# Half of two small tile loads moved from SyncE's queue to ScalarE's queue, in the column stage of a two-layer graph kernel

## What is computed

```python
# x is (5120, 64), adj is (5120, 5120), all float32
u = par_u[0] * par_u[1] * (diag_u[:, None] * x[:2048] @ W_u) + x[:2048]
i = par_i[0] * par_i[1] * (diag_i[:, None] * x[2048:] @ W_i) + x[2048:]
e = concatenate([u, i])
h = adj @ (adj.T @ e)
x = layernorm(x + layernorm(h) * gamma + beta + x)
T1 = adj @ x;  T2 = 2 * adj @ T1 - x;  T3 = 2 * adj @ T2 - T1
x = layernorm(x + x @ w[0] + T1 @ w[1] + T2 @ w[2] + T3 @ w[3] + bias)
```

## Time and profile before

| | before |
| --- | --- |
| median of 3 runs | 1223.32 us (1223.15 to 1223.8) |
| the profiled execution, its own time | 1222.88 us |
| its span, first to last instruction | 1221.1 us |
| PE busy | 1109.2 us (91%) |
| DVE busy | 928.5 us (76%) |
| ACT busy | 332.0 us (27%) |
| POOL busy | 257.0 us (21%) |
| HBM read | 348.97 MB, 287 GB/s over the span |

### The profile page before, as it was taken

The page is one execution under the profiler, slowest core; times in us unless marked ns, Lnnn a source line. Parts: engine busy times, 40 slices in busy tenths (PEclk is TensorE's granted clock), DMA queues, the critical chain, the costliest instruction groups (busy, mean ns, idle before and its releaser), DMA issues.

```text
span 1221.1 us, 13860 instructions
## 1 busy us (share of the span) xinstructions
PE 1109.2 (91%) x4995; PEld 480.7 (39%) x5004; DVE 928.5 (76%) x960; ACT 332.0 (27%) x594; POOL 257.0 (21%) x420
## 2 busy tenths in 40 slices
PE   4999999999999996899889999999899999598794
PEld 3444454444454442444333333444344443122221
DVE  2698798999998998698777766665666667588784
ACT  1456456466465562400100000000100000011010
POOL 0476555463453543100000000000000000011111
PEclk9999999999999998899999999999999999799898
DMA  7999999999999975899999999999999999999991
GB/s 225 301 291 299 278 299 305 297 295 282 300 274 288 282 206 121 181 291 309 238 347 347 337 313 308 306 293 255 262 331 333 325 305 328 348 311 342 352 353 33
DMA packets 372731, 350.82 MB, mean 287 GB/s; under 512 B 11613, under 2 KB 371333, under 8 KB 372693
## 3 DMA queue, kind: packets, MB, share of 16 engines
q1 hardware_dynamic: 259092, 237.35, 69.6%
q10 hardware_dynamic: 110880, 110.11, 31.6%
q0 software_dynamic: 2720, 2.86, 1.0%
HBM read 348.97 MB, written 1.31 MB: 287 GB/s over the span
## 4 chain that ended last, share of the span: by engine, by line
PE 54%; DVE 13%; SPq 12%; ACT 10%; ACTq 5%; issue 4%; DMA 1%; POOL 0%; DVEq 0%
PE bank L1176 30%; ACT terms L775 9%; SPq L337 7%; ACTq L279 5%; SPq L326 4%; DVE turned L496 4%; PE bank L1227 4%; PE bank L1189 3%; PE bank L1006 2%; PE bank L1046 2%; PE bank L1034 2%; PE bank L1018 2%; PE bank L1058 2%; DVE shared L516 2%; DVE xq L496 1%
## 5 line engine op out<-in xcount | busy, mean ns | idle before, releaser
L1176 PE MATMUL bank<-turned,terms 128*128 128x512 f32 x680 | 301.6, 596 | 4.8 <-DVE turned L496 3.3
L386 POOL COPY raw<-raw 32x512 f32<-32x512 f32 x320 | 194.2, 607 | 239.6 <-DVE raw L533 190.2
L516 DVE STREAM_TRANSPOSE shared<-shared 32x512 f32<-32x512 f32 x320 | 224.0, 700 | 4.1
L1006 PE MATMUL bank<-shared 128*64 128x256 f32 x1600 | 206.4, 385 | 6.9 <-DMA shared<-in_adj 6.9
L496 DVE STREAM_TRANSPOSE turned<-raw 128x2048 f32<-128x2048 f32 x72 | 165.1, 2301 | 58.3 <-PE bank L1176 49.5
L496 DVE STREAM_TRANSPOSE turned<-shared 128x2048 f32<-128x2048 f32 x68 | 156.1, 2303 | 60.6 <-PE bank L1176 46.4
L775 ACT COPY terms<-terms 32x512 f32<-32x512 f32 x320 | 197.0, 616 | 8.3 <-issue 3.2
L1176 PEld LDWEIGHTS bank<-turned,terms 128*128 128x128 f32 x680 | 126.6, 190 | 170.9 <-issue 163.3
L431 POOL DMA_DIRECT2D out<-scratch x40 | 21.7, 549 | 681.3 <-DVE scratch L725 681.2
L1006 PEld LDWEIGHTS bank<-shared 128*64 128x64 f32 x1600 | 112.0, 136 | 88.2 <-issue 32.6
L1069 PE MATMUL bank<-turned,t_quart 128*64 128x512 f32 x160 | 82.7, 603 | 8.5 <-DVE t_quart L540 8.5
(11 more groups left out here) (143 smaller groups left out, 1060.2 us busy)
## 6 DMA issues: line engine op xcount, KB each, us to landing
shared<-in_adj SPq DMA_DIRECT2D x100, 1024.0 KB, 10.8
raw<-in_adj SPq DMA_DIRECT2D x106, 512.0 KB, 10.6
raw<-in_adj ACTq DMA_DIRECT2D x106, 512.0 KB, 12.4
shared<-in_adj SPq DMA_DIRECT2D x104, 512.0 KB, 10.6
shared<-in_adj ACTq DMA_DIRECT2D x104, 512.0 KB, 12.6
raw<-in_adj SPq DMA_DIRECT2D x80, 256.0 KB, 7.6
xq<-in_x POOLq DMA_DIRECT2D x40, 32.0 KB, 6.2
out<-scratch POOLq DMA_DIRECT2D x40, 32.0 KB, 5.2
```

The source lines that it names most:

```text
L386: last = nc.gpsimd.tensor_copy(moved[Q32 * c:Q32 * (c + 1), :, :, Q32 * q:Q32 * (q + 1)], beside[Q32 * q:Q32 * (q + 1), :, c, :, :])
L516: last = nc.vector.transpose(low_turned[Q32 * c:Q32 * (c + 1), :, :, Q32 * q:Q32 * (q + 1)], low[Q32 * q:Q32 * (q + 1), :, :, Q32 * c:Q32 ...
L1006: last = nc.tensor.matmul(t_bank[H * odd:H * (odd + 1), 0:PW], e[:, s * SB + b, :], panels[slot][:, s * SB + b, :], start=(k == 0 and b < ...
L1176: last = nc.tensor.matmul(sum_bank[parity][:, :], terms[:, c * GB + i, columns], turned[place][:, i * BANK:(i + 1) * BANK], start=(first a ...
```

## The change

SP loads only the pieces q = 0 and 1 of each tile (partitions 0 to 63). The pieces 3 and 2 are issued by ScalarE's queue, in a new function `load_upper`. Before the loop ScalarE issues them for both tiles of the first pair, between the table load and panel 1. In the loop it issues them for both tiles of the next pair, behind the t copy of the even panel, after a wait on `tile_turned` for the tiles of the pair that is being used up. The counts that VectorE waits for are the same. `tile_rows` is moved up, so that both queues' code sees it.

```diff
--- before.py
+++ after.py
@@ -279,6 +279,8 @@
             queue.dma_start(pairs[u % SLOTS][Q32 * q:Q32 * (q + 1), :].rearrange("p (b n) -> p b n", b=GB * NQ),
                             rows_of[:, :, at_column:at_column + SPAN * P]).then_inc(pair_loaded[u % SLOTS], DMA)
 
+        tile_rows = adj.rearrange("(g b i) c -> g i b c", b=BANK // Q32, i=Q32)
+
         def by_chunk(a, width):
             return a.rearrange("p (k f) -> p k f", f=width)
 
@@ -316,13 +318,11 @@
 
             seg_rows = adj.rearrange("(s b p) c -> s p b c", p=P, b=SB)
 
-            tile_rows = adj.rearrange("(g b i) c -> g i b c", b=BANK // Q32, i=Q32)
-
             def load_layer0_tile(k, last, column):
 
                 if last is not None:
                     sp.wait_ge(tile_turned, last + 1 + RAW)
-                for q in (0, 2, 1, 3):
+                for q in (0, 1):
                     sp.dma_start(raw[k][Q32 * q:Q32 * (q + 1), :].rearrange("p (b c) -> p b c", c=P),
                                  tile_rows[2 * SEGS[k] + 1][:, :, bass.ds(column + P * q, P)])\
                         .then_inc(raw_loaded[k], DMA)
@@ -796,9 +796,22 @@
 
             act.wait_ge(ident_made, 2)
             nc.scalar.activation(stats[:, 1, 0:1], ident[:, 0:1], ACT.Sqrt)
+            def load_upper(k, last, column):
+
+                if last is not None:
+                    act.wait_ge(tile_turned, last + 1 + RAW)
+                for q in (3, 2):
+                    act.dma_start(raw[k][Q32 * q:Q32 * (q + 1), :].rearrange("p (b c) -> p b c", c=P),
+                                  tile_rows[2 * SEGS[k] + 1][:, :, bass.ds(column + P * q, P)])\
+                        .then_inc(raw_loaded[k], DMA)
+
+            for k in range(TILED):
+                load_upper(k, None, 0)
             layer0_panel(1, 1)
             with act.Fori(1, NJ // 2) as two:
                 layer0_panel(0, two * 2)
+                for k in range(TILED):
+                    load_upper(k, (two - 1) * TILED + k, two * BANK)
                 layer0_panel(1, two * 2 + 1)
 
             def take_h(n, s):
```

## The result

The change makes the kernel **slower**: 1237.72 us (median of 13 runs, 1228.07 to 1245.48) against 1224.22 us (13 runs, 1222.56 to 1226.54), a ratio of 1.0106 with a 95% interval of 1.0081 to 1.0131. The prediction was 1221.2 us with a range to 1226.2; the result lies outside it, on the other side.

A forecast was written before the change was run, and what follows sets the result against it. It took the column stage's early panels to be bound by DMA engines running behind, later ones by TensorE and ScalarE in turn. Settled lateness falling from 38.54 to 36.4 us took 2.1 off 1223.32: 1221.2 us, range 1220.2 to 1226.2.

The forecast's parts named there:

- A few us at most: Column stage: the change can only win back early transfer waits, 6.6 us in panels 1 to 6.
- the longest hold: Start of ScalarE's queue: bound with the longest issue, 5.2 us, giving panel 1 a lateness of 38.7, in all 1223.3 us.
- rival C: In the loop, ScalarE's issues hold it past the slack in every pair: 8 us slower, 1229.5 us; chance 0.15.
- the term for half a tile beside segments, 1.51 us: Early panels: two pieces, 524 KB, move beside SP's segments at 349 GB/s together, 0.88 us less than alone.
- rival B: Early panels: no overlap, panel 5 gets a half more ahead, 1225.3 to 1225.7 us; sign: panels 3, 5 later; chance 0.20.
- the prediction's terms for panels 1, 3 and 5: Lateness, t copy time minus 22.09 us per panel, from bytes ahead: 35.70, 35.32 and 35.27 us.
- ScalarE's hold at the start: Before the loop, four issues end at 41.96, so the first L766 copies and TensorE run 2.9 us late.
- the forecast's 36.4 for panel 1: Panel 1's lateness with the start's hold, 33.5 + 2.9; the largest term, so it sets the settled lateness, 38.54 before.
- the slack of 5.9: In the loop, the queue may hold ScalarE for 5.9 us after an even panel's t copy at no cost.
- A sign of being wrong in the reasons: Column stage: panel 1's copy isn't the one held back, or L1006 still waits for transfers in panels 5 and 6.
- should read near 349: Early stage: windows in which tile pieces run were to read near 349 GB/s and not 193.
- A: Column stage: the forecast as summed, with overlap, 2.1 us less, 1221.2 us (1220.4 to 1223.3 by hold); chance 0.50.

The follow-up runs named there:

- late: Tile 1's half issued behind the odd panel's t copy, against the change: 1253.92 us; the same with alternating pieces: 1229.66 us.
- amid the copies: Tile 1's half issued amid the odd panel's spread copies, against the change: 1232.44 us with alternating pieces, 1235.51 us with 0, 1 and 3, 2.
- one queue: SP issues all pieces in about the change's order, against the kernel before: 1244.58 us with 0, 1 and 3, 2; 1236.12 us alternating.
- the two named above: SP-only runs against the kernel before: pairs 0, 2 and 1, 3 one segment apart, 1233.87 us; 0, 1 and 3, 2 in the change's order, 1244.58 us.

## Why the prediction was wrong

**Right: the bound and the ceiling.** "A few us at most" holds (4.1 us with the tiles nearly gone), the settled pace didn't move, and what hurts in the change hurts in the first panels. Some bounds of the rivals are off by 0.1 to 0.2 us (38.54 - 35.70 off 1223.32 is 1220.5, the longest hold gives 1223.5, rival C 1229.3); none of them changes the forecast.

**Wrong: the term for half a tile beside segments, 1.51 us.** It measured 2.87 in the change (2.39 was its price alone). The 347 GB/s of the earlier trace rows were two queues with 1 KB packets, each into another group of 32 partitions. Here 512 B packets ran beside 1 KB packets, and the packet counts say what that gives: 3438 packets in 10 us of segments (row below), 344 per us, and 2814/8 = 352 per us with both queues. That is one large packet every 2.91 ns; of small ones alone one comes every 1/443 us = 2.26 ns (last section). Beside large ones a small one took 2.87/1043 us = 2.75 ns: none of its time was hidden behind the other queue's.

```profile
DMA packets 3438, 3.49 MB, mean 349 GB/s; under 512 B 60, under 2 KB 3435, under 8 KB 3435
```

The Trainium skill ("DMA: Bandwidth & Descriptors", Queues, rings and completion order) says that each DMA engine takes turns between the queues it has work for at packet granularity. The trace agrees that both queues move at once between 92 and 100 us. It doesn't show turns of one packet each (1770 and 1043), and at 484 to 489 us the second queue moved nothing. The same page's rule that spreading over queues gains no bandwidth (Rules for kernel authors), which I had set aside on the earlier trace rows, held here.

In the run with alternating halves the queues between 90 and 98 us read

```profile
q1 hardware_dynamic: 1791, 1.81, 81.6%
q10 hardware_dynamic: 1166, 0.58, 29.8%
```

or 8.0 - 1.81/0.349 = 2.81 us for 0.58 MB, 2.5 for a half (2.4 ns per packet). That is about the 2.39 of a half alone: rival B had the price, no overlap, nearly right. With 2.5 in place of 1.51 the prediction's terms for panels 1, 3 and 5 become 35.07 - 2.39 + 2 x 2.5 = 37.7, 36.45 - 3 x 2.39 + 4 x 2.5 = 39.3 and 38.16 - 5 x 2.39 + 6 x 2.5 = 41.2. That run has 37.50, 39.86 and 44.14: the one size put right gives panels 1 and 3 and leaves 2.9 us of panel 5, of which 1.7 are the low clock (below). In the change, with its 2.87, they become 38.4, 40.8 and 43.4 against 37.96, 43.66 and 51.24. Most of the growing rest is the next point.

**Wrong: a part of the change that no term covered.** The sum took the two pieces as two pieces, whichever. Going from 0, 2 and 1, 3 to 0, 1 and 3, 2 is 8.5 of the 13.5 us. Four pairs of runs that differ in nothing else show it beyond their intervals: 1237.7 and 1229.2 (both halves), 1227.7 and 1224.3 (tile 0), 1234.8 and 1227.0 (tile 1), 1253.9 and 1229.7 (late). Two more point the same way with intervals that overlap: 1235.5 and 1232.4 (amid the copies), 1244.6 and 1236.1 (one queue). The order alone, in the kernel before, costs 2.2 us. So *that* the order of pieces costs is shown; *why* is argued. That the partition halves 0 to 63 and 64 to 127 matter rests on rows of one stretch, 134 to 169 GB/s against over 182, and the alternating run on one queue has a low of 139. An open rival is what the pieces read: 0 and 1, and 3 and 2, are also neighbouring columns of the same rows of adj, and no run here changes which columns go to which partitions. For the partition halves the Trainium skill has a reason ("SBUF — State Buffer", Door 1: The DMA port swizzle): partitions 32 apart share a port and partitions 64 apart don't, so a transfer to 64 neighbouring partitions reaches no more ports than one to 32. By it pieces 0 and 1 queue at the same eight ports. The rates of that stretch fit, but no run here shows a port.

**Wrong: the price of an order.** The sum and rival B counted the bytes ahead of a segment. ScalarE's pieces overtake part of SP's backlog, so their place by issue says little (early 1229.2, late 1228.9). Pieces right behind a segment seem to delay it too (55.02 for 52.87, in one comparison), and on one queue pieces between segments cost 9 us that no count of bytes gives.

**Missed: what a long wait costs behind it.** Behind TensorE's longer waits the granted clock often read 0.50 for some 3 us: in the change at 43 to 46 us behind the wait of 2.20, at 101 to 104 behind 2.63, and at 153 to 158 with waits of 2.64 and 2.50; in its alternating version at 149 to 152 behind 2.17. Not always: behind that version's wait of 2.30, at 101.83, it stayed at 1.00. It costs only where no later wait takes it up, on the last segment of a panel: 1.5 us in the change and 1.7 in its alternating version (148.61 to 154.59, 5.98 for 4.29), both in panel 5. The kernel before has no such stretch between 57 and 170 us. In the one-queue run, behind a wait of 4.14 us, it is the lower level too:

```profile
54.63 3.68 PE L1010 MATMUL bank<-shared 128*64 128x256 f32 x16 [4.14 <-DMA shared<-in_adj]
...
56.00:60.00 4.00, 2.78 (x14) 1.20 (x12) 0.00 (x0) 0.00 (x0) 0.00 (x0) 0.50 1.03 252
```

This may also be part of why the changed kernel's runs spread over 17 us and those of before over 4. Its slower runs do have the lower mean clock (0.978 and 0.976 in the two fastest, 0.968 in the two slowest), which doesn't say which causes which.

**Right in size, wrong in effect: ScalarE's hold at the start.** The first copy was forecast at 41.96 and came at 41.84. Part of that is luck: the burst took 4.47 us instead of 4.33, and began at 37.27, ahead of the table load. But the forecast's 36.4 for panel 1 let this hold decide, as if the transfers no longer would. It didn't decide. Panel 1's t comes 4.29 us behind the start on the last segment, as before, and that start moved from 52.87 to 55.76, the whole 2.89 us. The hold of 2.2 us, and the matmuls at the low clock behind it, are over before. In the loop the first pairs hold ScalarE for 5 us and the slack of 5.9 took that. Rival C fell.

**The signs.** Panels 3 and 5 later than 102.72 and 148.61 were to mean B. They are, and the side was B's and nearly the price of a half, but its 2.0 to 2.3 us were neither the whole cause nor the size. A sign of being wrong in the reasons came too: L1006 waits for transfers in panel 5 more than before, 2.50 us for its last segment alone against 1.12. The windows that "should read near 349" read 196 to 290: the sign against A was the right one to name.

**Open.** Why the order of the pieces costs; why pieces between segments on one queue cost 9 us; and 1.2 us of panel 5's lateness with alternating halves, which is within what two executions differ by. Behind panel 19 the change has 763.6 us to the end of the span against 761.9 before. The other runs, without the two named above, have 760.4 to 765.0 there, so these 1.7 us need no cause. No version beat the kernel before; the best, tile 0's half alone and alternating, equals it.

## What to carry to other kernels

A second queue moves no more beside transfers that already keep the engines busy, and small packets on it cost there at least what they cost alone. It also overtakes part of the first queue's backlog, so a load issued there can land ahead of what was issued before it. When a transfer is split into groups, treat the sequence of the groups as part of the design and read a diff for the order as closely as for the bytes; here alternating between partitions 0 to 63 and 64 to 127 was the better order. And before you add up delays, look for the last thing that is waited for: a hold or a slow stretch ahead of it costs nothing.

## What the runs showed of the hardware

- Neighbouring groups of 32 partitions, which are neighbouring columns too: 211 GB/s for a tile alone against 219 alternating; beside segments, in the one stretch compared, 134 to 169 against 182 and more.
- Two queues with 512 B and 1 KB packets: 352 packets per us in the change and 2958/8 = 370 in its alternating version, against 344 with 1 KB packets alone. 512 B packets alone reach 1329/3 = 443 per us:

```profile
DMA packets 1329, 0.66 MB, mean 219 GB/s; under 512 B 48, under 2 KB 1329, under 8 KB 1329
```

- TensorE's granted clock: 0.50 for some 3 us behind idle times of 2.17 to 2.63 us, but not behind each (2.30 in the alternating version left it at 1.00); the 16 matmuls of a segment then take 3.4 us and not 1.95.

- A burst of four issues on ScalarE held its sequencer for 4.1 to 5.0 us while SP had a backlog, and 3.1 to 3.3 us in the settled pace:

```profile
275.21 3.14 ACTq L804 DMA_DIRECT2D raw<-in_adj  x4
...
319.39 3.33 ACTq L804 DMA_DIRECT2D raw<-in_adj  x4
```
